# The second gather sum of a graph kernel: two of every 64 gathered tiles are fetched row by row by SyncE and ScalarE

## What is computed

```python
ht = jnp.einsum('ne,reh->rnh', hidden, weights[l])
msg_f = ht[edge_type, src] + biases[l][edge_type]
out = jax.ops.segment_sum(msg_f, dst, num_segments=n_nodes)
msg_b = ht[edge_type + n_rel, dst] + biases[l][edge_type + n_rel]
out = out + jax.ops.segment_sum(msg_b, src, num_segments=n_nodes)
x = _layernorm(x + out)
```

## Time and profile before

| | us |
|---|---|
| median of three runs | 5433.64 (5424.72 to 5434.58) |
| the profiled execution, time | 5436.53 |
| its span, first to last instruction | 5434.8 |
| first gather sum (3149 to 4290 of the span) | 1141 |
| second gather sum (4290 to 5411) | 1121 |
| residual, norm and output after it | 23.8 |

### The profile page before, as it was taken

How to read it: one execution, slowest core, us unless ns; L and a number is a source line. 1 busy time by engine, 2 the same in 40 slices (tenths; PEclk the granted TensorE clock), 3 DMA queues, 4 the chain that set the end, 5 groups by cost and what they waited for, 6 DMA issues and landing times. The chain is left out here.

```text
span 5434.8 us, 50013 instructions
## 1 busy us (share of the span) xinstructions
PE 3062.4 (56%) x13750; PEld 2237.6 (41%) x13751; DVE 2231.2 (41%) x2709; ACT 614.3 (11%) x1076; POOL 3413.0 (63%) x3213
## 2 busy tenths in 40 slices
PE   3899989567777777744918633343333333333333
PEld 1788879233333333324917422232222323232223
DVE  7999985445555454568901331111111111101112
ACT  0455540000000000004701000000000000000000
POOL 2888868466556555657770356666666666666664
PEclk7999999666666666657958766665665656555555
DMA  5566667144444444425825332222222111111111
GB/s 177 157 181 192 177 198 230 37 131 138 132 133 139 132 135 130 139 87 159 259 62 195 136 100 70 69 64 60 60 59 60 48 46 46 45 46 46 46 46 46
DMA packets 498663, 599.91 MB, mean 110 GB/s; under 512 B 190115, under 2 KB 367441, under 8 KB 496248
## 3 DMA queue, kind: packets, MB, share of 16 engines
q0 software_dynamic: 117856, 246.12, 16.5%
q1 hardware_dynamic: 337751, 229.77, 14.8%
q10 hardware_dynamic: 42944, 122.68, 6.0%
HBM read 406.69 MB, written 204.36 MB: 112 GB/s over the span
## 5 line engine op out<-in xcount | busy, mean ns | idle before, releaser
L720 POOL DMA_INDIRECT rec_by_src<-rec,pos x782 | 1123.3, 1436 | 524.6 <-issue 238.9
L1132 PE MATMUL ps<-g_got,g_hot 128*128 x3224 | 687.5, 367 | 1225.8 <-issue 797.4
L1132 PEld LDWEIGHTS ps<-g_got,g_hot 128*128 128x128 f32 x3224 | 605.7, 272 | 1320.2 <-issue 1318.9
L1592 POOL DMA_INDIRECT sc_kv<-kv,d_src x806 | 761.8, 945 | 533.9 <-DVE sc_kve L1644 260.2
L1032 POOL DMA_INDIRECT g_got<-y_forward,d_msg x782 | 739.3, 945 | 381.8 <-issue 230.1
L1032 POOL DMA_INDIRECT g_got<-y_back,s_msg x782 | 737.8, 943 | 381.2 <-issue 233.5
L805 PE MATMUL ps<-ln_low,ln_hot 128*125 128x256 f32 x2848 | 620.3, 381 | 20.3 <-DVE ln_low L782 16.1
L805 PEld LDWEIGHTS ps<-ln_low,ln_hot 128*125 128x125 f32 x2848 | 535.6, 188 | 104.8 <-issue 24.4
L1043 DVE TENSOR_TENSOR g_hot<-ps,src_loc 128x1024 f32<-128x1024 f32 x101 | 120.6, 1221 | 992.5 <-remote 450.4
L1699 PE MATMUL ps<-w_e,sc_attrT 128*128 128x512 f32 x404 | 320.0, 887 | 246.0 <-ACT sc_attrT L1611 216.3
L1051 DVE TENSOR_TENSOR g_y<-ps,ms_b 128x384 f32<-128x384 f32 x75 | 41.8, 558 | 808.8 <-remote 474.2
(11 more groups left out here) (323 smaller groups left out, 3283.7 us busy)
## 6 DMA issues: line engine op xcount, KB each, us to landing
linked<-ln_out SPq DMA_DIRECT2D x320, 224.0 KB
ve<-sc_kve ACTq DMA_DIRECT2D x202, 256.0 KB
wv_ve<-ve SPq DMA_DIRECT2D x101, 512.0 KB
l_links<-linked SPq DMA_DIRECT2D x25, 800.0 KB
l_links<-linked ACTq DMA_DIRECT2D x25, 800.0 KB
f_links<-linked SPq DMA_DIRECT2D x25, 800.0 KB
f_links<-linked ACTq DMA_DIRECT2D x25, 800.0 KB
attr_pairs<-ln_feats POOLq DMA_DIRECT2D x7, 2048.0 KB
```

Of the source, the lines that this page charges most:

```text
L720: pool.indirect_dma_start(out=dram["rec_by_src"], out_offset=bass.IndirectOffsetOnAxis(ap=S["pos"][:, c:c + 1], axis=0), in_=S["rec"][:, c ...
L1132: last = pe.matmul(ps[:, bass.ds(columns[j], width)], hot[:, q, j, :], got[:, bass.ds(slots[j], width)], start=False, stop=True, skip_grou ...
L1592: pool.indirect_dma_start(out=kv[:, q, j, :], out_offset=None, in_=dram["kv"], in_offset=bass.IndirectOffsetOnAxis(ap=S["d_src"][:, c:c + ...
```

## The change

In the second call alone, two of every 64 tiles are no longer gathered by POOL. They are the last tile of the fourth group in a round of the ring (ACT's) and the last of the eighth (SP's), over 12 rounds, which makes 24 of 782 tiles. For such a tile ACT or SP reads the row numbers from `s_rows`, eight at a time into registers, and issues one DMA of one row, 512 bytes, for each of the 128 edges (`fetch_rows`). The rows go into a buffer `aside` with two halves. DVE waits for the 128 rows and copies the half into the tile's slot in the ring (`hand`), behind the `compare` of the same group. PE waits for this copy beside the seven gathers. A helper starts its first two tiles when the call begins, and each later one when DVE has handed over the tile before the last.

In the first call, DVE makes a copy `s_rows` of the row numbers, and the six copies out of PSUM that ACT made are now DVE's (`place`). ACT's writes of `y_back` no longer stand behind them. The row numbers are worked out six groups later (`NAMED_AT` 36 for 30), and the steps are turned one group earlier (`FLIP_AT` 5 for 6).

```diff
-def gather_sum(nc, S, dram, tag, name, table, index, fresh=True, back=False):
+def gather_sum(nc, S, dram, tag, name, table, index, rows, fresh=True, back=False):
+    HELPERS = {} if back else {"act": RING // 2 - 1, "sp": RING - 1}
+        aside = {e: m.sb(f"{tag}_aside_{e}", [P, 2 * D]) for e in HELPERS}
...
-            CLIMB_AT, ROWS_AT, FLIP_AT, LOCAL_AT, NAMED_AT, ROWS_BEFORE = 3, 8, 6, 24, 30, 8
+            CLIMB_AT, ROWS_AT, FLIP_AT, LOCAL_AT, NAMED_AT = 3, 8, 5, 24, 36
...
+        def tile_of(e, k):
+            return k * SLOTS + HELPERS[e] * GROUP + GROUP - 1
+
+        helped = {tile_of(e, k) for e in HELPERS for k in range(WHOLE)}
+
+        def fetch_rows(eng, e, kind, i, h, lo, hi):
+            p = tile_of(e, h)
+            for at in range(lo, hi, GROUP):
+                _, named = nc.values_load_multi_w_load_instructions(
+                    rows[p:p + 1, bass.ds(i * P + at, GROUP)], engines=[kind], min_val=0, max_val=ROWS * RELATIONS - 1,
+                    skip_runtime_bounds_check_because="row numbers are node times relations plus type")
+                for j in range(GROUP):
+                    eng.dma_start(aside[e][at + j:at + j + 1, h * D:(h + 1) * D],
+                                  table[bass.ds(named[j], 1), :]).then_inc(fetched_rows[e][h], 16)
...
+        def rows_alone(eng, e, kind):
+            for h in range(2):
+                fetch_rows(eng, e, kind, 0, h, 0, P)
+            with eng.Fori(1, WHOLE // 2) as i:
+                for h in range(2):
+                    eng.wait_ge(handed[e], i * 2 + (h - 1))
+                    fetch_rows(eng, e, kind, i, h, 0, P)
...
-                keep_rows(act, 1, 0, ROWS_BEFORE)
-                for n, (array, k, lo, hi) in enumerate(flats):
-                    act.wait_ge(flat, n + 1)
-                    act.activation(array[:, lo:hi], free[:, 0:hi - lo], ACT.Copy).then_inc(placed, 1)
-                keep_rows(act, 1, ROWS_BEFORE, BLOCKS)
-                act.wait_ge(placed, len(flats))
+                tables(act, 1, 0, BLOCKS)
+            else:
+                rows_alone(act, "act", mybir.EngineType.Activation)
...
                 for c in range(g * GROUP, min((g + 1) * GROUP, TILES)):
+                    if c in helped:
+                        continue
...
+            def hand(e, h, count):
+                at = tile_of(e, 0) * D
+                dve.wait_ge(fetched_rows[e][h], count)
+                dve.tensor_copy(got[:, at:at + D], aside[e][:, h * D:(h + 1) * D]).then_inc(handed[e], 1)
+
+            def place(n):
+                array, k, lo, hi = flats[n]
+                dve.wait_ge(flat, n + 1)
+                dve.tensor_copy(array[:, lo:hi], free[:, 0:hi - lo]).then_inc(placed, 1)
...
+                dve.wait_ge(built, 2)
+                dve.tensor_copy(S["s_rows"][:, :], wide[:, 1, 0:HELPED * P]).then_inc(copied, 1)
...
-                with dve.Fori(0, WHOLE) as i:
-                    for k in range(RING):
+                with dve.Fori(0, WHOLE // 2) as i:
+                    for k in range(2 * RING):
...
+                        for e in helper_of(k):
+                            hand(e, k // RING, (i + 1) * (16 * P))
...
-                    pe.wait_ge(landed[k], i * (16 * GROUP) + 16 * lands)
+                    own = k in HELPERS.values()
+                    pe.wait_ge(landed[k], i * (16 * (GROUP - own)) + 16 * (lands - own))
+                    for e in helper_of(k):
+                        pe.wait_ge(handed[e], i + 1)
```

More of the change, by code:

```diff
@@ L72 @@
 BANK = 512
+HELPED = 6
 assert 2 * GROUP * (RING - 4) >= BLOCKS - 1 + GROUP and PAIRS_PAD % 24 == 0 and PAIRS_PAD + 2 * GROUP <= PAIR_COLS and BLOCKS % CHUNK == 0 and TILES % (2 * SCAT) == 0
@@ L934, in gather_sum @@
     WHOLE, REST = divmod(GROUPS, RING)
+    HELPERS = {} if back else {"act": RING // 2 - 1, "sp": RING - 1}
+    QUARTER = P // 4
+    assert WHOLE % 2 == 0 and SLOTS * 2 == P and WHOLE * SLOTS <= HELPED * P
     with ExitStack() as stack:
@@ L937, in gather_sum @@
         got = m.sb(tag + "_got", [P, SLOTS * D])
+        aside = {e: m.sb(f"{tag}_aside_{e}", [P, 2 * D]) for e in HELPERS}
+        fetched_rows = {e: [m.sem(f"{tag}_rows_{e}{h}") for h in range(2)] for e in HELPERS}
+        handed = {e: m.sem(f"{tag}_handed_{e}") for e in HELPERS}
         hot = m.sb(tag + "_hot", [P, WAYS, GROUP, P])
@@ L972, in size, with helper_of, tables, keep_rows @@
             return min(GROUP, PAIRS - n * GROUP)
-        def keep_rows(eng, k, first, last):
+        def helper_of(n):
+            return [e for e, k in HELPERS.items() if n < WHOLE * RING and n % RING == k]
+        def tile_of(e, k):
[10 more added lines that the diff above has]
+                                  table[bass.ds(named[j], 1), :]).then_inc(fetched_rows[e][h], 16)
+        def tables(eng, k, first, last):
             for b in range(first + k, last, 2):
-                eng.wait_ge(biased, (b + 1) * PIECES)
-                eng.dma_start(dram["y_back"][b * P:(b + 1) * P, :], y[:, k, :]).then_inc(saved[k], 16)
+                keep_rows(eng, k, b)
             if last == BLOCKS:
                 eng.wait_ge(saved[k], 16 * ((BLOCKS + 1 - k) // 2))
+        def rows_alone(eng, e, kind):
[5 more added lines that the diff above has]
+                    fetch_rows(eng, e, kind, i, h, 0, P)
+        def keep_rows(eng, k, b):
+            eng.wait_ge(biased, (b + 1) * PIECES)
+            eng.dma_start(dram["y_back"][b * P:(b + 1) * P, :], y[:, k, :]).then_inc(saved[k], 16)
         @block.sync
@@ L998, in _ @@
                 sp.dma_start(tile_rows[0:rest, full, :], by_src[full * P:TILES, :]).then_inc(carried, 16)
-                keep_rows(sp, 0, ROWS_BEFORE, BLOCKS)
+                tables(sp, 0, 8, BLOCKS)
                 sp.wait_ge(filed, 16)
+            else:
+                rows_alone(sp, "sp", mybir.EngineType.SP)
         @block.scalar
@@ L1096, in _ @@
                         bias(beside[n - 1])
+                    for e in helper_of(n):
+                        k = n // RING
+                        hand(e, k % 2, (k // 2 + 1) * (16 * P))
+                    if n - 1 in flat_at:
+                        place(flat_at[n - 1])
                     if n == CLIMB_AT:
@@ L2279, in gnn_kernel @@
             S["src_steps"] = r.sb("src_steps", [1, 3 * PAIR_COLS], I32)
+            S["s_rows"] = r.sb("s_rows", [P, HELPED * P], I32)
             with ExitStack() as third:
@@ L2285, in gnn_kernel @@
                 norm_and_messages(nc, S, dram)
-                gather_sum(nc, S, dram, "g3", "dst", tables[0], S["d_msg"], back=True)
-            gather_sum(nc, S, dram, "g4", "src", tables[1], S["s_msg"], fresh=False)
+                gather_sum(nc, S, dram, "g3", "dst", tables[0], S["d_msg"], None, back=True)
+            gather_sum(nc, S, dram, "g4", "src", tables[1], S["s_msg"], S["s_rows"], fresh=False)
         residual_norm(nc, S, dram, "n3", False, out=out)
```

10 lines of the change are left out of this document (6 added, 4 removed).

## The result

The changed kernel takes 5908.43 us (median of 6 runs, 5894.23 to 5923.41), the kernel before beside it 5433.01 us (6 runs). The ratio is 1.0881, with a 95% interval of 1.0868 to 1.0895: 475 us slower. The profiled execution has a span of 5904.0 us.

The account below looks back on a forecast made before the run. The second gather sum was taken as bound in turns by POOL's gather issuing and PE's slow stretches. Of 30.0 us for 24 gathers half arrives, helpers cost nothing: 5433.6 - 15.2 = 5418.4, say 5418 us; range 5400 to 5455.

Parts of the forecast that it names:

- rival 4: Second sum: helpers too slow and set the round, from a row at 0.61 us on; kernel 5503 or 5655 us; chance 0.20.
- the row fetch at 0.45 us and the tile at 68 us: SP and ACT in the second sum: one row DMA with surroundings 0.45 us, a tile 68 us, between 44 and 81.
- The cover: Helpers' slack in a ring round of about 89 us: 8 to 45 us, gone at a row of 0.61 us.
- 1280 such steps keep their medians: Argument against slow helpers: SP's register instructions and moves have medians of 0.04 and 0.03 us, though longest 0.69 and 0.70.
- The half on the path: Second sum: POOL's issuing is on the path 34.4 of 68.1 us, so 15.2 of 30.0 us saved arrives.
- Rival 2: Second sum: all 30 us of saved issue time arrives, kernel 5404 us; chance 0.10.
- The start: Start of the second sum: ACT's first tile takes 68 us, PE starts 26 us late; counted as nothing, 26 kept for range.
- The long loop body: Helpers' loop of at least 544 rows, fetched again: must cost over 40 us in each of five passes to matter.
- the first sum: First gather sum: six copies moved from ACT to DVE and the copy `s_rows`, counted as nothing.
- the copies on DVE: Second sum: 24 copies of 128x128 at 0.3 us, 7 us on an engine idle for 1000.
- the sign shown for case 4: Second sum, if helpers are too slow: SP or ACT busy without pause, PE waiting for `got` behind DVE's copy every fourth group.
- The formula of case 4: Second sum if helpers are too slow: 12 tiles plus about 70 us for the groups behind the last one.

Follow-up runs that it names:

- pool_memsets: Changed kernel with six of eight gathers in each group of the second sum replaced by POOL's writes of zeros to a spare tile; 5147.44 us, ratio 0.9500.
- before_gap_128: Kernel before, with a POOL write of zeros to a 128x128 spare tile behind each gather in both sums; ratio 1.0020.
- no_rows: Changed kernel with the 24 tiles fetched by nobody, their slots zeros, and helpers, copies and their waits gone; 5398.70 us, ratio 0.9947.
- rows_32: Changed kernel with each helper fetching only the first 32 of a tile's 128 rows, the others zeros; 5405.16 us, ratio 0.9957.
- one_in_four: Changed kernel with each helper fetching one whole tile in four rounds, 6 tiles in all, POOL gathering 776; run twice, ratios 1.0013 and 1.0015.
- constant_addresses: Changed kernel with as many row DMAs from constant addresses (wrong rows), without register loads, register instructions and moves; 5454.08 us, ratio 1.0042.
- pool_light: Changed kernel with POOL gathering only two of eight tiles of each group in the second sum, the others read as zeros; 5252.81 us, ratio 0.9676.

## Why the prediction was wrong

The forecast was 5418, the result 5908: rival 4, to which it gave 0.20.

*The step that failed* is the row fetch at 0.45 us and the tile at 68 us, with bounds of 44 and 81, and with it the overlap: "both keep up ... and cost nothing after the start". While POOL stands still the price is nearly right, 0.52 us a row and 67 us a tile. While POOL gathers it is 4.5 us a row. In a round POOL issues 62 gathers in 77 us; by the working 17 rows fall into them, and the other 111 follow at 0.52 us, 135 us in all, against 132 measured and 89 that were there. Counted in SP's records, 20 rows of a round take more than 1.6 us each, 66 us together, and the other 108 take 66 us as well. The cover was to be gone at 89 us.

*Why the rows misled.* All prices of a row came from windows in which POOL did not gather at this rate: the earlier trace rows from the first 7 us, from 160 to 784. The register load alone was read beside the gathers, and its longest was 1.39 us where the median was 0.59. The argument "1280 such steps keep their medians" was made in the wrong neighbourhood. The earlier trace rows were the only rows from the right one, with one engine at 2.8 us a matmul record beside unbroken gathers, and they spoke for the rival. Its price was too low as well: it reckoned with 0.65 or 0.75 us a row, and the mean was 1.03.

*The half on the path* was wrong too, though it is not what moved the time by 475 us. It took PE's slow stretches as a period of their own that POOL fills, so that less issuing would turn into longer stops. In fact the stretches come with POOL's back-to-back gathers (pool_memsets, before_gap_128). With 24 gathers less the stops stay at 130 to 135 us, and all of the 30 us arrives within the noise (no_rows, 28.8). Rival 2 had this at 0.10.

*The start.* ACT's first tile was 137 us after the begin, not 68, and the loss went on in every round; the start was no separate case.

*The long loop body.* The prediction said that fetching it again had to cost over 40 us in each of five passes to matter. It costs about 2.5 us in each of four returns, so leaving it out of the sum was right.

*What held:* the first sum (0.9997), the copies on DVE (0.23 us each) at nothing, PE's additional waits, for which no run shows a cost, POOL's 758 gathers at 1.25 us, and the sign shown for case 4: helpers without a pause to the end, and PE waiting for `got` behind DVE's copy. The formula of case 4, with the measured 132 us for a tile, gives 1654 us and is 54 us too long, by its 70 us for the tail. The hardware queues had room, as the sum had it: at full pace, from 4370 to 4410, the row fetches take 0.8% of 16 engines.

The row fetches took the hardware path (the packets of its queue q1 go from 337751 to 340823), and were slowed by GpSimd's gathers from 0.52 to 4.5 us a row. The Trainium skill, "DMA: Bandwidth & Descriptors", section "SWDGE vs HWDGE vs iDMA", says that DMAs issued through the hardware path are immune to the interference that GpSimd's descriptor rings suffer from VectorE. No run here shows that interference, and what slowed the row fetches comes from GpSimd and not from VectorE; on that the sentence says nothing.

What stays open is where the instructions wait. That back-to-back gathers bring the slow pace, and that it goes with their distance, is shown. Whether they wait on the way to the engine, or for something in its sequencer, no run here tells.

## What to carry to other kernels

Price work for an idle engine from rows that stand beside the neighbours it will have, not from its best rows elsewhere: beside an unbroken sequence of gathers 1.25 us apart an instruction on SP or ACT costs 1.40 us, so count instructions, not DMAs or bytes. An idle engine next to a POOL that gathers without a break has room for some 30 rows, or 100 instructions, in 77 us and a short stop (rows_32), and even that was not always free (one_in_four, 0.3%). If two engines change pace in the same moment that a third stops, take the third for the cause first, and test it by leaving out its work.

## What the runs showed of the hardware

- Beside indirect gathers on POOL 1.17 to 1.25 us apart, SP and ACT get one instruction every 1.40 us, each with a record of 0.70 us, whether it is a register instruction, a move or a DMA. At 1.45 us apart a row of 3.25 instructions takes 0.8 us on average, at 2.1 us 0.52 us, which is the undisturbed pace. POOL's memsets do nothing of the kind.
- The slow pace doesn't begin at once. Counted in the trace's records behind the first 14 returns of POOL, SP does about 12 instructions and ACT about 25 at full pace first (medians; single values for SP spread from 0 to 28), in some 3 and 5 us. In constant_addresses, where an instruction takes longer on average, it is about 14 and 27, in some 5 and 9 us. The number stays nearly the same and the time does not, which looks like a store of instructions that runs empty; no run here tests that.
- Nor does it end at once, and the more gathers went before, the longer it lasts. In the change's trace it ends some 3 us behind the start of the last gather after 7 gathers in a row, 4 us after 16, 4 to 6 us after 23 to 31, and 11 us after the first 62. The gathers' own packets start no later than 2.3 us behind the start of the last gather in four of these stops (those behind 4356.2, 4451.0, 4509.4 and 4636.3), so it is not their data that the instructions still wait for. It looks like a backlog that the gathers leave; what it consists of no run tells.
- A return to the start of a loop body of two tiles (some 830 records) costs SP and ACT 2.4 to 2.5 us (pool_light), and 0.2 to 0.7 us where the body is a quarter as long (rows_32).
- PE has the same slow stretches, but later, mostly behind 70 records or more. In the kernel before they are what makes PE late, and POOL stops for 135 of 1121 us.
